# Gates carried in the rows, transposing loads, adding gathers and three parts in a routed feed-forward layer

## The reference, cut to what matters

```python
x = x + xattn(layernorm(x), ctx, w_q, w_kv, w_out, b_out)
x2 = layernorm(x); logits = x2 @ router_w.T          # 8 experts
_, idx = top_k(softmax(logits), 2)
gate[token, idx] = logits[token, idx]                # the raw logits are the gates
for e in range(8):
    h = silu(x2 @ w1[e].T) * (x2 @ w3[e].T)          # 176 hidden
    moe += gate[:, e:e+1] * (h @ w2[e].T)
moe += (silu(x2 @ sw1.T) * (x2 @ sw3.T)) @ sw2.T     # the shared expert
x = x + moe
```

## Time and profile before

| | us |
|---|---|
| median of 3 runs (lowest, highest) | 1151.36 (1148.72, 1157.14) |
| the profiled execution, its own time | 1156.14 |
| its span, first to last instruction | 1153.5 |
| PE busy in the span | 954.7 (83%) |
| DVE busy | 892.4 (77%) |
| ACT busy | 690.0 (60%) |
| POOL busy | 758.7 (66%) |

### The profile page before, as it was taken

How to read it: one execution, slowest core, us unless ns; L and a number is a source line. 1 busy time by engine, 2 the same in 40 slices (tenths; PEclk the granted TensorE clock), 3 DMA queues, 4 the chain that set the end, 5 groups by cost and what they waited for, 6 DMA issues and landing times.

```text
span 1153.5 us, 29498 instructions
## 1 busy us (share of the span) xinstructions
PE 954.7 (83%) x10016; PEld 775.8 (67%) x10016; DVE 892.4 (77%) x2026; ACT 690.0 (60%) x1454; POOL 758.7 (66%) x1052
## 2 busy tenths in 40 slices
PE   5857899999999998999996999884868887676655
PEld 5555778887887777787884887664757775543333
DVE  4666689998988887898998897883666767786676
ACT  3544678777777766676774676662647764453222
POOL 2232567558778767777787577767765257787775
PEclk9878899999999999999998899996889999897776
DMA  8051233423444432332333443552444444452242
GB/s 261 4 153 30 42 53 74 128 53 72 68 66 72 70 61 56 70 74 59 75 72 61 81 70 62 78 130 50 130 128 141 128 125 129 115 143 78 79 137 73
DMA packets 209711, 102.39 MB, mean 89 GB/s; under 512 B 143488, under 2 KB 201504, under 8 KB 208576
## 3 DMA queue, kind: packets, MB, share of 16 engines
q1 hardware_dynamic: 201376, 83.72, 33.2%
q0 software_dynamic: 8192, 16.79, 5.2%
HBM read 39.65 MB, written 31.46 MB: 62 GB/s over the span
## 4 chain that ended last, share of the span: by engine, by line
PE 42%; issue 12%; POOL 12%; DVE 11%; DMA 10%; another core or an unknown queue 6%; ACT 4%; SPq 1%; DVEq 1%; POOLq 0%; ACTq 0%
DMA OT_lo<-O_lo 8%; PE Q L1219 5%; PE S L1153 5%; PE W L1093 4%; POOL O_lo L511 4%; PE W L1095 4%; PE W L1094 3%; PE W L1106 3%; PE W L1108 3%; PE W L1107 2%; DVE X L1059 2%; PE S L1206 2%; PE S L1207 2%; POOL rstd L456 1%
## 5 line engine op out<-in xcount | busy, mean ns | idle before, releaser
L961 DVE TENSOR_TENSOR pt_lo<-Q,pt_hi 77x512 f16<-77x512 f32 x256 | 164.5, 680 | 41.3 <-ACT pt_hi L622 40.5
L511 POOL TENSOR_TENSOR O_lo<-O,O_hi 128x512 f16<-128x512 f32 x128 | 146.5, 1164 | 33.6 <-ACT O_hi L630 18.5
L622 ACT ACTIVATE pt_hi<-Q 77x512 f16<-77x512 f32 x256 | 144.5, 590 | 27.2 <-PE Q L1219 25.8
L431 POOL DMA_INDIRECT xs<-x2cat,pos x128 | 134.8, 1053 | 31.1 <-issue 31.1
L538 POOL DMA_INDIRECT Yr<-ys,pos_y x128 | 125.9, 983 | 42.4 <-issue 32.0
L1219 PE MATMUL Q<-ident,P 128*77 128x128 f32 x1024 | 150.8, 281 | 1.7 <-ACT P L605 1.1
L1153 PE MATMUL S<-G,xTm 128*128 128x462 f32 (+1 forms) x384 | 145.3, 514 | 0.6 <-ACT G L612 0.6
L1206 PE MATMUL S<-v_hi,pt_hi 96*128 96x65 f16 x1024 | 109.3, 199 | 31.2 <-DVE P L930 28.8
L1219 PEld LDWEIGHTS Q<-ident,P 128*77 128x77 f32 x1024 | 124.6, 152 | 3.3 <-issue 1.7
L1206 PEld LDWEIGHTS S<-v_hi,pt_hi 96*128 96x128 f16 x1024 | 96.5, 99 | 41.5 <-DVE P L930 33.8
L1106 PE MATMUL W<-wo_hi,OT_hi 128*128 128x128 f16 x512 | 92.7, 224 | 36.9 <-DMA OT_lo<-O_lo 35.3
(11 more groups left out here) (211 smaller groups left out, 3287.9 us busy)
## 6 DMA issues: line engine op xcount, KB each, us to landing
xg<-xs SPq DMA_DIRECT2D x80, 128.0 KB
ys<-ysb SPq DMA_DIRECT2D x40, 256.0 KB
xp<-x2cat SPq DMA_DIRECT2D x64, 64.0 KB, 1.5
xg<-xp SPq DMA_DIRECT2D x16, 256.0 KB
y_out<-X SPq DMA_DIRECT2D x16, 256.0 KB
X<-x_in SPq DMA_DIRECT2D x1, 2304.0 KB, 10.2
xs<-x2cat,pos POOLq DMA_INDIRECT x128
xs<-zero_in SPq DMA_DIRECT2D x16, 128.0 KB, 2.5
```

Of the source, the lines that this page charges most:

```text
L431: pool.indirect_dma_start(out=xs_d[0 if b < PART[0] else 1][:, :], out_offset=index(pos, b, k), in_=x2cat[:, b % RING, :], in_offset=None) ...
L511: pool.tensor_tensor(O_lo[:, half_], O[:, (t + 1) % 2, half_], O_hi[:, half_], ALU.subtract).then_inc(s["p_Olo"], 1)
L622: act.activation(pt_hi[0:NK, j % 2, c * 512:(c + 1) * 512], QB[q_bank(j, c)][0:NK, :], ACT.Copy).then_inc(s["a_PThi"], 1)
L961: dve.tensor_tensor(pt_lo[0:NK, j % 2, c * 512:(c + 1) * 512], QB[q_bank(j, c)][0:NK, :], pt_hi[0:NK, j % 2, c * 512:(c + 1) * 512], ALU.s ...
```

## The change

- **Three parts** of 24, 24 and 16 batches in place of two. Each part is padded to whole granules per expert, so there are 16, 16 and 12 routed items (44 in place of 40), and 60 items in all.
- **Gates in the rows.** DVE scales the gates when a chunk of 8 batches is chosen. POOL writes the gate behind the row (`set_gate`; a row now has 264 two-byte numbers), once for each of the token's two scatters; the second scatter goes one slot later.
- **Loads by transposing DMAs.** SP loads each granule straight into `xT` with a transposing DMA, and its 256 gates with a small DMA of their own. PE's `rows_turn` and DVE's `turned` are gone.
- **y gated at evacuation.** The result is multiplied by the gates when it leaves PSUM: even items on ACT in four pieces, odd items on DVE. `down` alternates between banks Q0 and W2.
- **Gathers add into X**: an indirect DMA that adds; `mix` and the ring `Yr` are gone. The gathers come four batches at a time in every second iteration, first all first rows, then all second rows.
- The low half of hA is made on POOL for the first 16 items and on DVE after that.
- **Tables in six pieces**, one a slot, and the edges are cleared after that.
- **Projection last in the slot** on PE, and DVE's `residual` first in the next slot. The shared items start with the last part's batches. In the feed-forward iterations the tail slots come last on ACT and DVE.

```diff
-PART = [40, 24]
+PART = [24, 24, 16]
...
+        gathers = {}
+        b, n = 0, ROUTED[0] + LAG + 2
+        while b < NB:
+            ready = sum(PART[p] for p in range(NP) if first_of(p + 1) + LAG + 2 <= n)
+            take = [v for v in range(b, min(b + 4, ready))] if n % 2 == 0 else []
+            gathers[n] = take
...
             def load_rows(n):
                 if n >= XG:
-                    wait(sp, "f_T", n - XG + 1)
...
+                    wait(sp, "f_B", n - XG + 1)
...
+                    if n >= 4:
+                        sp.wait_ge(s[f"gr{n % 4}"], 32 * (n // 4))
+                    if n >= GR:
+                        y_out(sp, n - GR)
                     at = nc.values_load_multi_w_load_instructions(
...
                     for q, v in enumerate(at):
-                        sp.dma_start(xg[:, n % XG, 2 * q:2 * q + 2, :],
-                                     xs_d[p][ds(v, GRAN), :].rearrange("(i p) n -> p i n", p=128)).then_inc(ring, 16)
+                        rows = xs_d[p][ds(v, GRAN), :]
+                        sp.dma_start(to[:, :, q * GRAN:(q + 1) * GRAN].bitcast(U16), rows[:, 0:2 * D], transpose=True).then_inc(ring, 16)
+                        sp.dma_start(gates[:, n % GR, 2 * q:2 * q + 2, :],
+                                     rows[:, 2 * D:2 * D + 2].rearrange("(i p) n -> p i n", p=128)).then_inc(s[f"gr{n % 4}"], 16)
...
-                if t == TAB_SLOT[0]:
-                    clear_edges(0)
+                if t - TAB_PIECES in TAB_SLOT:
+                    clear_edges(TAB_SLOT.index(t - TAB_PIECES))
...
+            def set_gate(b, k):
                 pool.wait_ge(s["p_pos"], b // CB + 1)
...
+                    pool.wait_ge(s[f"sc{b % RING}"], 32 * (b // RING) + 16)
+                col = k * CB + b % CB
+                pool.tensor_copy(x2cat[:, b % RING, 2 * D:2 * D + 2].bitcast(F), best[:, b // CB, col:col + 1]).then_inc(s["p_gate"], 1)
...
-            def gather(b):
-                p = 0 if b < PART[0] else 1
-                wait(pool, "e_mix", 2 * (b - YR + 1))
-                for k in range(2):
-                    pool.indirect_dma_start(out=Yr[:, b % YR, k, :], out_offset=None, in_=ys_d[p][:, :],
-                                            in_offset=index(pos_y, b, k)).then_inc(s[f"ga{b % YR}"], 16)
+            def gather(b, k, n):
...
+                    pool.wait_ge(s[f"ga{b % 8}"], 32 * (b // 8) + 16)
+                pool.indirect_dma_start(out=X[:, b, :], out_offset=None, in_=ys_d[p][:, :],
+                                        in_offset=index(pos_y, b, k), compute_op=ALU.add).then_inc(s[f"ga{b % 8}"], 16)
...
-                act.activation(ysb[:, m % 3, :], WB[2][:, :], ACT.Copy).then_inc(s["g_y"], 1)
+                act.wait_ge(s[f"gr{m % 4}"], 32 * (m // 4 + 1))
+                for i in range(GB):
+                    cols = slice(i * D, (i + 1) * D)
+                    last = act.activation(ysb[:, m % 3, cols], y_bank(m)[:, cols], ACT.Copy, scale=gates[:, m % GR, i, :].bitcast(F))
+                last.then_inc(s["g_y"], 1)
...
+                if on(t, 3, NB + 3):
+                    residual(t - 1)
                 if on(t, 0, NB):
                     piece_max(0); piece_max(1); piece_sub(0); piece_max(2); piece_sub(1); piece_sub(2)
...
-                if on(t, 2, LAST):
-                    residual(t)
...
-            turned(0)
-            last_it = max(NI + LAG + 1, n_end + 2)
-            for n in range(last_it):
-                if LAST + n <= TAIL:
-                    slot(LAST + n)
-                if n + 1 < NI:
-                    turned(n + 1)
...
+            for n in range(NI + LAG + 2):
                 if on(n - 1, 0, NI):
                     low_C(n - 1)
+                if on(n - 1, LOW_POOL, NI):
+                    low_A(n - 1)
+                if on(n - LAG - 1, 0, NR) and (n - LAG - 1) % 2 == 1:
+                    result_out(n - LAG - 1)
+                if on(n - LAG - 1, NR, NI):
+                    shared_add(n - LAG - 1 - NR)
                 if n < NI:
                     hidden_C(n)
                     hidden_A(n)
...
-                if on(t, 2, LAST):
-                    project(t)
                 if any(turns(t)):
                     turn(t)
                 if gon:
                     g_piece(3)
                 if now:
                     p_turn(2); p_turn(3)
+                if on(t, 2, LAST):
+                    project(t)
```

More of the change, by code:

```diff
@@ L249, in stored, with gathered, y_out, shared_at @@
         def stored(eng, b):
-            wait(eng, f"xp{b % RING}", 16 * (b // RING + 1))
-        def part_of(n):
-            return 0 if n < ROUTED[0] else 1
+            wait(eng, f"xp{b % 4}", 16 * (b // 4 + 1))
+        def gathered(eng, b):
+            wait(eng, f"ga{b % 8}", 32 * (b // 8 + 1))
+        def y_out(eng, m):
+            wait(eng, "g_y", m // 2 + 1)
+            wait(eng, "e_y", (m + 1) // 2)
+        def shared_at(b):
+            return NR + ORDER.index(b // GB) + LAG
+        def part_of(n):
+            return sum(n >= sum(ROUTED[:p + 1]) for p in range(NP - 1))
+        def first_of(p):
+            return sum(ROUTED[:p])
+        def batch_part(b):
+            return sum(b >= sum(PART[:p + 1]) for p in range(NP - 1))
+        def y_bank(m):
+            return (QB[0], WB[2])[m % 2]
+        gathers = {}
[4 more added lines that the diff above has]
+            gathers[n] = take
+            b += len(take)
+            n += 1
+        n_end = n
+        gather_at = {b: n for n, some in gathers.items() for b in some}
+        OUT_ORDER = sorted(range(NS), key=lambda i: max(NR + i + LAG, gather_at[ORDER[i] * GB + GB - 1]))
+        LOW_POOL = ROUTED[0]
         block = stack.enter_context(nc.Block())
@@ L466, in x_loaded, with slot @@
                 eng.wait_ge(s[f"ld_x{max(k for k in range(4) if XP[k] <= b)}"], 16)
-            def slot(t):
+            def slot(t, tail=None):
                 if on(t, -1, NB - 1):
@@ L486, in slot @@
                     pool.tensor_tensor(xb[:, (t + 1) % 2, :], X[:, t - 1, :], bo[:, :], ALU.add).then_inc(s["p_xb"], 1)
-                if on(t - S_SCATTER, 0, NB):
-                    scatter(t - S_SCATTER)
+                scatters(t)
                 if chunk_of(t, S_PLACE) is not None:
                     members(chunk_of(t, S_PLACE))
+                if tail is not None:
+                    tail()
                 if on(t - 4, 0, NB):
@@ L723, in _ @@
                     gate_A(n)
+                if n > 0 and LAST + n <= TAIL:
+                    slot(LAST + n)
         @block.vector
@@ L1076, in _ @@
                     hidden_A(n)
-                if on(n - LAG, NR, NI):
-                    shared_add(n - LAG - NR)
-                for b in gathers.get(n - 1, ()):
-                    mix(b, min(max(n - LAG - NR + 1, 0), NS))
+                if n > 0 and LAST + n <= TAIL:
+                    slot(LAST + n)
         @block.tensor
@@ L1281, in up_C @@
             def up_C(n, pieces_n):
-                wait(pe, "e_T", n + 1)
+                pe.wait_ge(s[f"xg{n % XG}"], sum(32 if m < NR else 16 for m in range(n % XG, n + 1, XG)))
                 if n == 0:
@@ L1334, in _ @@
                     up_A(n, pcs[n])
-                    if n == 0:
-                        project(LAST)
+                if any(turns(LAST + n)):
+                    turn(LAST + n)
+                if n == 0:
+                    project(LAST)
+                if n < NI:
                     up_B(n, pcs[n])
```

324 lines of the change are left out of this document (166 added, 158 removed).

## The result

The changed kernel took **1243.01 us** (median of 4 runs, 1240.84 to 1253.86), the kernel before 1151.57 on the same chip: ratio 1.081 [1.074, 1.087] (the brackets are a 95% interval), slower where I forecast 1046. The profiled execution took 1253.86 us with a span of 1252.1, so it stands 10.9 us above the median. Medians here are over all runs of a version, while ratios leave out single executions that were over 1.5% above their version's fastest; that concerns one of e12 and two of e10, the profiled ones among them.

What follows compares the result with a forecast made beforehand. PE was taken to bound attention, and gathers to cost the feed-forward items most (85 us). 760 + 18 + 73 + 124 + 57 + 12 = 1044, POOL's lane 1046, plus 2: span 1048, median 1046 us; range 1000 to 1110.

Steps and rivals of the forecast that it cites:

- Attention −30: Attention slots: projection last and tables in pieces save 30 of 41 us lost, bounds +8 and −41.
- change of stage −12: Between attention and routed items: PE's other order in slot 64 saves 12 of 37 us, bounds 0 and −17.
- The waits, −24: Attention: the moved projection removes some 24 us of PE's 35.3 us of waits for the turned low half.
- attention gives nothing: Rival for attention: DVE, at 9.2 of 10.2 us, takes the place of the turned half; 1076 us, chance 0.06.
- Twelve pieces of tables, 0.3 us each: Attention: 12 table pieces of about 1.3 us in 12 slots, charged 0.3 us each, 3.6 for 10.4.
- Routed item 4.6: Routed items: SP is the limit at 4.4 us, taken as 4.6 with jitter; 27 items make 124 us.
- The slower rival: Rival for routed items: the transposing load from DRAM costs 2.3 us an issue, total over 1163 us; chance 0.07.
- Items 0 to 17: Routed items beside the scatters, bound by POOL: first three 18 us, the other 14 at 4.75 each.
- The clearing, 6.5: Clearing the third part's edges: 6.5 us added, 5.53 of it SP's, with nothing to hide it.
- Gathers 1.25 us each: POOL's 128 gathers cost 1.25 us each, between 1.25 and 1.6 if adding costs more.
- the rival with POOL last: Rival at the end: adding gathers at 1.6 us each are the last lane, 1074 us; chance 0.09.
- TensorE's clock +2: Over the span: 2 us added for a lower granted clock, as PE would be busy 3.2 of 4.6 us.

Runs made afterwards that it cites:

- e12: The changed kernel itself, measured a third time, on a chip of the slower kind: 1248.17 us, 1.080 against the kernel before.
- e10: The changed kernel with two parts of 40 and 24 batches in place of 24, 24 and 16: 1273.69 us, 1.097 against the kernel before.
- e14: The kernel before with only the low half of hA moved from POOL to VectorE from item 26 on: 1110.09 us, 0.977.
- e5: The changed kernel itself, measured again on a chip of the faster kind: 1186.06 us, 1.042 against the kernel before.
- e13: The kernel before with only the projection last in PE's slot and the residual first in DVE's, run again on a faster chip: 1122.61 us, 0.988.
- e2: The kernel before with only the projection last in PE's slot and the residual first in DVE's: 1125.52 us, 0.990.
- e17: The kernel before with only the projection last and the residual first, one run on a slower chip: 1221.46 us, kernel before 1150.36.
- e6: The changed kernel with plain loads in place of transposing ones, shared items too: 1153.32 us, 1.015 against the kernel before.
- e7: The changed kernel without the gate loads and SP's wait for them, all gates 1: 1155.78 us, 1.016 against the kernel before.
- e4: The changed kernel with gathers that write X instead of adding to it: 1142.32 us, 1.006 against the kernel before.

## Why the prediction was wrong

**Attention −30 and change of stage −12: gave about 2 us on one kind of chip, minus 62 on the other.** On the first kind e14 has the old attention (first item product at 800.2) and e5 the new one (797.9). Three terms failed there.

- *The waits, −24: gave 9.* The wait for the turned half did go, as I said (8.7 us in e5). But only 26.2 of the 35.3 us of the earlier trace rows lie in the 141 to 765 that I summed, the longest wait not among them, and I took the floor of 10.4 us for safe once that wait was gone. In the new order PE waits some 0.35 us for pt_lo in every slot, 22.9 us in all (e13), and the slot is 10.85. That is my rival *attention gives nothing* (0.06) in kind, VectorE in the place of the turned half.
- *Twelve pieces of tables, 0.3 us each: took some 1.6.* Above 10.83 us a slot the first six slots with pieces cost 8.6 us in e5 and the next five 9.7. The one table in one piece cost 20.1 + 12.0 − 21.7 = 10.4 in e2. I had changed 10.4 for 3.6 and got 18.
- *Change of stage, −12: gave 4* (36.7 in e14, 32.6 in e5).

Some 4 us more lie in the first eight slots (slot 3 takes 16.6 us in e5, 11.8 in e2), and no run tells why.

The remaining 67 us on the slower chips come from the order: with nothing else changed e17 has its first item product at 870.3, the kernel before at 802.8. The step of the prediction that failed is the moved projection. I asked what covers VectorE's residual, and that held (in e13 VectorE still waits 0.22 us for the scores behind it), but I put at nothing what the projection itself had covered. **The cover was PE's own projection**, 396.23 − 394.89 = 1.34 us of matmuls that had stood between pt_lo and the turn and absorbed any lateness: from 150 to 640 us the old order shows no wait for pt_lo at all, in the kernel before as in e14. Nothing in the trace of before could have given 67 us, but the slot of the earlier trace rows, PE at 10.20 of 10.20, said that no slack was left behind it.

**Routed item 4.6: took 6.4.** SP was named as the limit, rightly, and its lane was mis-sized, 5.8 against 4.4. The transposing issue was put at 0.85, between "half the size" and the earlier trace rows; it is 1.20, the same as for twice the size. That is 0.7 an item. Each small load of gates costs 0.43 and some 0.30 to pass on, 1.46 for two where I had 0.93 (0.5), and the way from the store to the loads 1.95 instead of 1.78 (0.2). Of the rest, 0.6 us in the first run, 0.4 is the clearing in item 17, spread over 27 items, and the others are issues that were held, for which I had charged 0.2. PE's 3.2 us can't be checked behind this, but e6's 4.4 us an item shows that nothing else bounds above that. VectorE's new low half took 0.69 us (median of 44, longest 0.76) in the first run, and 38 of them lay beside a gather on POOL by the trace's times: the hold by a gather that I had allowed for didn't come. The slower rival (transposing load dear, 0.07) gave the right direction and the wrong threshold: it asked for 2.3 us an issue, while 1.2 sufficed beside other losses.

**Items 0 to 17: 102 to 104 instead of 84.5, the clearing left out.** The first three took 17 to 19 us, as forecast; the other 14 took 6.1 each and not 4.75. I had let POOL alone bound them, and SP's queue of 5.8 us stands above that: in e5 SP waits for only 0.6 us from 815 to 885. With the shorter queues of e6 and e7 the same items still took 5.6 and 5.7. What bounds them there is not settled. One part of it is that POOL's second gate waits until the first scatter has landed (10 waits, 7.9 us, in those 70 us of e5), which I had put into 0.1 us an item.

**The clearing, 6.5: took some 10.** Item 17 took 15.7 us in the first run against 6.1 for the items around it, because SP's full queue leaves nothing to hide it.

**Gathers 1.25 us each: took 1.85.** I had the range 1.25 to 1.6 and took the lower end although no row showed an adding gather; even the upper end was too low. From the first to the last of the 128 it is 245 us in the first run (995.5 to 1240.7) and 249 in e5 (927.3 to 1176.7, with one wait of 11.7 for stored results), and this lane ends last. The rival with POOL last (0.09, 1074) was right in kind. In e5 it decides the end: with fast items (e6) the span falls to 1149.7 and no further.

**TensorE's clock +2: not seen on the path.** In routed items the granted clock was 0.80 in the first run and 0.83 in e5, and there PE was busy 111 us for what took some 87 in e6. But PE had room: its items came at SP's pace. No run separates the clock from that pace.

My range (1000 to 1110) excluded all of it because each lane was priced at its lower or middle value, and the lanes were treated as exclusive rivals; SP's and POOL's were late together. On the faster kind of chip, without the slow slots, the changed kernel still takes 1186 us.

## What to carry to other kernels

Count a queue's lane by the issue, not by the bytes: two transposing issues and two small ones raised SP's item from the 2.5 us that I read before to 5.8, and no engine was full. Before a block of work is moved, ask who was covered by it; a slot with no hole has no room for what stands behind the moved block, and a version that gains 1% on one chip can lose 6% on the next of the same type, so such an edit is timed on more than one. When a loop's pace is one engine's (here POOL's gathers beside its subtraction), moving one operation to an engine with room was worth 2.3% [1.9, 2.7] (e14).

## What the runs showed of the hardware

- The issue of a transposing DMA didn't shrink with its size: 1.20 us (median of 88) for 128 KB from DRAM in the changed kernel, 1.26 (median of 16) for 256 KB from DRAM, and 1.23 for 256 KB from SBUF; a plain one takes 0.37. The loads of the shared items, first run (min/median/max ns):

```profile
L362 SPq DMA_TRANSPOSE xT<-xp x16: 1225/1260/2063, 1134.4 to 1182.4; - x16
```

- An adding gather takes POOL 1.54 us instead of 0.95, and it moves in other packets. Queue 0 in items 18 to 44, in e5 (74 gathers), then in e4 (84): packets, MB, share of the engines.

```profile
q0 software_dynamic: 10237, 4.66, 27.0%
```

```profile
q0 software_dynamic: 2644, 5.44, 14.4%
```

- The chips met here fall into two kinds for this kernel, 1134 to 1138 and 1150 to 1152 us, and the difference of 1% in the kernel before becomes 5% in the changed kernel (1186 against 1243 to 1248) and 9% with the projection last alone (1123 against 1221). Where TensorE's late results at a granted clock of 1.00 come from stays open, and so does whether e14's gain of 2.3% holds on the slower kind: it was not run there.
